# Scores of the two 16-wide attention layers: from 64x64 parts of the matmul array with four-head keys to 32x64 parts with two-head keys

## What is computed

```python
# layer 0
energy = jnp.einsum('bhqd,bhkd->bhqk', q, k)
att = jax.nn.softmax(energy, axis=-1) / D ** 0.5
out = jnp.einsum('bhqk,bhkd->bhqd', att, v)
# layer 3: the same with rotary q and k, and scores / sqrt(16)
```

## Time and profile before

| | us |
|---|---|
| runs | 2855.83, 2855.84, 2857.46 |
| median | 2855.84 |
| profiled execution, span from first to last instruction | 2859.8 |
| layer 0, tiles 5 to 28 (about) | 75 to 294 |
| layer 3, steady tiles | 2243 to 2468 |
| TensorE busy, whole span | 2583.2 (90%) |
| VectorE busy | 1614.8 (56%) |
| ScalarE busy | 1050.9 (37%) |
| GpSimd busy | 486.5 (17%) |
| mean granted TensorE clock | 0.962 of full |

### The profile page before, as it was taken

One profiled execution on the slowest core, in us unless ns is written; L12 is line 12 of the kernel. 1 busy time (PEld: TensorE's weight loads), 2 busy tenths in 40 slices (PEclk: granted clock), 3 DMA queues, 4 the chain that ended last, 5 costly groups with the idle time before them and its releaser, 6 DMA issues.

```text
span 2859.8 us, 60211 instructions
## 1 busy us (share of the span) xinstructions
PE 2583.2 (90%) x24161; PEld 1815.8 (63%) x24161; DVE 1614.8 (56%) x3691; ACT 1050.9 (37%) x2104; POOL 486.5 (17%) x407
## 2 busy tenths in 40 slices
PE   6888599999999946997999999997998888799999
PEld 5666366666666644665888888884444677556555
DVE  6999778787878773122455555443333677722221
ACT  4555365555555501211333333332121666411110
POOL 2223110101010103332111111110000656400000
PEclk9999899999999957998999999998998999999999
DMA  5000000000000032434100000000000233200000
GB/s 203 2 2 2 12 23 22 29 22 29 22 29 22 19 97 95 129 104 112 48 0 0 0 0 0 0 1 1 0 0 0 86 95 97 60 8 15 7 15 15
DMA packets 72121, 101.90 MB, mean 36 GB/s; under 512 B 10864, under 2 KB 50288, under 8 KB 71472
## 3 DMA queue, kind: packets, MB, share of 16 engines
q1 hardware_dynamic: 65840, 91.46, 10.0%
q0 software_dynamic: 6144, 8.56, 1.5%
HBM read 67.20 MB, written 32.80 MB: 35 GB/s over the span
## 4 chain that ended last, share of the span: by engine, by line
PE 79%; DVE 13%; issue 3%; ACT 2%; DMA 1%; POOL 1%; another core or an unknown queue 0%; SPq 0%; DVEq 0%; ACTq 0%
PE psW L320 16%; PE psW L313 8%; PE psS L1322 7%; PE psP L435 4%; PE psP L1288 4%; PE psP L428 4%; PE psP L1282 4%; PE psS L1316 4%; PE psO L1282 4%; PE psO L1288 4%; PE psS L379 3%; PE psO L412 3%; PE psO L344 2%; PE psW L528 2%; PE psP L395 2%
## 5 line engine op out<-in xcount | busy, mean ns | idle before, releaser
L320 PE MATMUL psW<-r,work 128*128 128x512 f32 x1024 | 481.6, 604 | 1.0 <-DVE work L755 1.0
L1218 POOL TENSOR_TENSOR work<-work 128x512 f32<-128x512 f32 x128 | 132.1, 1043 | 1141.8 <-DVE work L777 1141.7
L320 PEld LDWEIGHTS psW<-r,work 128*128 128x128 f32 x1024 | 180.6, 191 | 162.4 <-issue 156.8
L313 PE MATMUL psW<-work,r 128*128 128x128 f32 x2048 | 244.2, 278 | 1.0 <-DVE work L755 1.0
L313 PEld LDWEIGHTS psW<-work,r 128*128 128x128 f32 x2048 | 235.6, 193 | 3.5 <-DVE work L755 1.4
L766 DVE TENSOR_REDUCE work<-psS 128x8 f32<-128x512 f32 x256 | 175.4, 685 | 92.6 <-PE psS L558 55.8
L1322 PE MATMUL psS<-r,work 128*128 128x256 f32 x960 | 211.2, 381 | 5.3 <-DVE work L1385 5.3
L1322 PEld LDWEIGHTS psS<-r,work 128*128 128x128 f32 x960 | 181.2, 190 | 32.8 <-DVE work L1385 6.1
L768 DVE TENSOR_TENSOR work<-psS,work 128x512 f32<-128x512 f32 x256 | 176.9, 691 | 11.3
L1138 ACT ACTIVATE work<-work 128x512 f32<-128x512 f32 x128 | 80.1, 626 | 276.4 <-DVE work L768 276.4
L1196 POOL TENSOR_TENSOR work<-work,head_mask 128x1024 f32<-128x1024 f32 x64 | 121.2, 1894 | 207.0 <-ACT work L1074 204.5
(11 more groups left out here) (271 smaller groups left out, 4656.7 us busy)
## 6 DMA issues: line engine op xcount, KB each, us to landing
r<-in_l_fc SPq DMA_DIRECT2D x16, 1024.0 KB
rotated<-work SPq DMA_DIRECT2D x60, 256.0 KB
work<-mod_rows SPq DMA_DIRECT2D x64, 128.0 KB, 2.8
work<-rotated SPq DMA_DIRECT2D x30, 256.0 KB
r<-in_l_w SPq DMA_DIRECT2D x2, 3072.0 KB, 19.2
x<-in_x SPq DMA_DIRECT2D x8, 512.0 KB, 9.2
gather_table<-work SPq DMA_DIRECT2D x32, 128.0 KB, 1.8
moe_sum<-work SPq DMA_DIRECT2D x32, 128.0 KB, 1.7
```

Of the source, the lines that this page charges most:

```text
L313: ins = nc.tensor.matmul(ps[:, q * P:(q + 1) * P], w[:, k, lo + q * P:lo + (q + 1) * P], L.hT[:, k, :], start=(k == 0), stop=(k == KC - 1))
L320: ins = nc.tensor.matmul(ps[:, 0:width], L.hT[:, k, :], w[:, k, lo:lo + width], start=(k == 0), stop=(k == KC - 1))
L1218: nc.gpsimd.tensor_tensor(E, E, halves(L.rs)[i].unsqueeze(2).broadcast_to([P, 8, N]), ALU.mult).then_inc(L.s[f"prob{i}"].sem, 1)
```

## The change

The scores of layers 0 and 3 are computed on 32x64 parts of the array. One matmul now takes 32 partitions (two heads, "group" 0 to 3) and one sequence as weights and streams 128 columns: the 64 keys twice, each copy zeroed except for one of the two heads. That is 16 matmuls a tile where there were 8, each with half the rows and half the columns. The four groups write four banks: groups 0 and 1 the two banks of psP, groups 2 and 3 the two banks of psS, 256 columns in each. Since psP also receives the transposed probabilities, the scores of tile t now also wait for ptb of tile t-1.

`kbd` is halved (128x512), and so is its multiplication on GpSimd, which now takes its two 0/1 columns from `par`. VectorE has a softmax of its own for these layers: each of its four instructions takes the same 512 elements a partition as before, 256 from each of two banks (psP for the first half, psS for the second). The order of heads in E, and with it `narrow_pairs`, changes accordingly.

```diff
-                    self.kbd = [W.take(4, 4, N) for _ in range(2)]
+                    self.kbd = [W.take(4, 2, N) for _ in range(2)]
...
             for ch in range(KC):
-                for rh in range(2):
-                    for i in range(2):
-                        yield rh * 4 + ch * 2 + i, ch, rh * 2 + i
+                for group in range(4):
+                    yield group * 2 + ch, ch, group
...
                 after(pe, L.s["mask"], t + 1)
                 after(pe, L.s["sub1"], t)
+                after(pe, L.s["ptb"], t)
                 for ch in range(KC):
                     for b in range(2):
-                        for rh in range(2):
-                            rows, at = slice(64 * rh, 64 * rh + 64), rh * 512 + ch * 256
-                            bb = b ^ rh
-                            ins = nc.tensor.matmul(psS[64 * bb:64 * bb + 64, at:at + 256],
+                        for group in range(4):
+                            rows, bb = slice(32 * group, 32 * group + 32), b ^ (group % 2)
+                            ins = nc.tensor.matmul((psP, psS)[group // 2][64 * bb:64 * bb + 64, group % 2 * 512 + ch * 128:
+                                                                          group % 2 * 512 + ch * 128 + 128],
                                                    L.qk[t % 2][rows, ch, bb * N:(bb + 1) * N],
                                                    L.kbd[t % 2][rows, 2 * ch + bb, :, :], start=True, stop=True)
-                            if ch == KC - 1 and b == 1:
-                                ins.then_inc(L.s[f"s{rh}"].sem, 1)
+                            if ch == KC - 1 and b == 1 and group % 2:
+                                ins.then_inc(L.s[f"s{group // 2}"].sem, 1)
...
+        def dve_narrow_softmax(v, ch, L, t):
+
+            for i, ps in enumerate((psP, psS)):
+                ps = ps[:, :].rearrange("p (s a b) -> p s a b", s=2, b=N)[:, :, 0:4, :]
+                mx = halves(L.mx)[i].rearrange("p (s a) -> p s a", s=2)
+                after(v, L.s[f"s{i}"], t + 1)
+                ch.link(nc.vector.tensor_reduce(mx, ps, AX.X, ALU.max))
+                after(v, L.s["tb" if i else "ta"], t)
+                nc.vector.tensor_tensor(L.E[:, 8 * i:8 * i + 8, :].rearrange("p (s a) b -> p s a b", s=2), ps,
+                                        mx.unsqueeze(3).broadcast_to([P, 2, 4, N]), ALU.subtract
+                                        ).then_inc(L.s[f"sub{i}"].sem, 1)
...
-                nc.gpsimd.tensor_tensor(L.kbd[n % 2], k.unsqueeze(2).broadcast_to([P, 4, 4, N]),
-                                        head_mask[:, 8:12].unsqueeze(1).unsqueeze(3).broadcast_to([P, 4, 4, N]),
+                nc.gpsimd.tensor_tensor(L.kbd[n % 2], k.unsqueeze(2).broadcast_to([P, 4, 2, N]),
+                                        par.unsqueeze(1).unsqueeze(3).broadcast_to([P, 4, 2, N]),
                                         ALU.mult).then_inc(L.s["mask"].sem, 1)
```

More of the change, by code:

```diff
@@ L827, in dve_narrow @@
                 ch.reset()
-                dve_softmax(v, ch, L, t)
+                dve_narrow_softmax(v, ch, L, t)
                 if t > 1:
```

## The result

The changed kernel takes 2823.70 us (median of four runs, 2819.75 to 2826.11); the kernel before took 2856.65 us beside it (four runs, 2855.83 to 2859.12). The ratio is 0.988, with an interval of [0.9867, 0.9893]. Forecast were 2821 us, a range of 2797 to 2840, and 0.91 for faster. The profiled execution of the changed kernel took 2819.75 us, so it is the fastest of the four; its span is 2817.9.

What follows compares the result with a forecast made beforehand. VectorE, held by GpSimd's mask, bounds layer 0; TensorE's chain bounds layer 3. Savings of 20.4 + 2 + 12.6 = 35 us take the span from 2859.8 to 2824.8, median 4.0 lower: 2821 us, range 2797 to 2840.

Steps and rivals of the forecast that it cites:

- What bounds: Layer 0: VectorE, 96% busy, its normalisation held by GpSimd's mask, period 9.20 us; layer 3: TensorE's chain, 8.32 us.
- The mask: Layer 0: GpSimd's product falls to 1.04 us, VectorE's normalisation ends 0.85 us earlier in 24 tiles, 20.4 us.
- The ends of layer 0: The other eight tiles of layer 0: 0.4 us each for five, nothing for three; 2 us, bounds 0 and 5.
- The scores: Layer 3: eight parts at once cut the scores from 1.02 to 0.60 us; 0.42 in 30 tiles, 12.6 us.
- The sum: Whole kernel: 20.4 + 2 + 12.6 = 35 us saved, giving 2821 us, 1.2% less.
- Late next: Layer 3: whether VectorE becomes limiting; 0.85 of its 1.31 us wait before the softmax used up, 0.5 left.
- The edits at no cost: Wait for ptb, two-bank softmax halves, layer 3 mask, new narrow_pairs order: free, at worst 5 us over layer 0.
- A: Layer 3: only four parts work at once, so scores gain nothing; 22.4 us in all, 2833 us; chance 0.14.
- C: Layer 0 gains less: mask costs 1.28 us or two-bank softmax is slower; 24 to 29 us, 2829; chance 0.12.
- D: Scores slower: 32-row parts do not overlap, 3.7 us; layer 3 loses 80 us, layer 0 30; 2965; chance 0.05.
- E: Layer 0: the mask is not the cause of the 2.12 us normalisation; only 13 to 15 us remain, 2842; chance 0.03.
- B: Layer 0: normalisation escapes the mask after a 0.1 us shift, VectorE's loop 7.5 us; 56 us, 2800; chance 0.08.

Runs made afterwards that it cites:

- one column half: Changed kernel, but from tile 1 of each narrow layer all 16 score matmuls write the lower 64 partitions, four parts instead of eight; 2834.91 us, ratio 0.9920.
- half mask: Kernel before with its old scores, GpSimd masking only two of four head copies (512 elements) from tile 2 on; 2834.62 us, ratio 0.9926.
- the changed kernel again: Changed kernel unaltered, measured a second time beside the kernel before; 2819.25 us, ratio 0.9868.
- norm early: Layer 0's normalisation L743 moved ahead of the statistics, before the mask starts: on the changed kernel 2807.26 us, on the kernel before 2844.22 us.

## Why the prediction was right, point by point

**What bounds.** Both readings held. VectorE stays at 95% in layer 0, and TensorE's chain stays whole in layer 3. TensorE's loop in layer 0, put at 7.0 us, is the 7.08 to which tiles 25 to 28 fall once VectorE no longer binds. The two halves of the change, run alone, gave 20.9 us in layer 0 and 12.0 in layer 3 and add up to the whole; the prediction had costed them as two kernels in one, 22.4 and 12.6.

**The mask.** Taken was 1.04 us, from a product of as many elements with an operand that is constant inside; measured 1.040. The term 24 x 0.85 = 20.4 is 217.7 - 197.3 = 20.4 in the traces (tiles 5 to 28). The normalisation was expected at 1.27 and stands at 1.266 to 1.272 in 24 of 24.

**The ends of layer 0.** The estimate of 2 us was too low: the other seven intervals between scores went from 58.4 to 54.9, 3.5 us. It is the one term of the sum that was clearly mis-sized, within its bounds of 0 and 5.

**The scores.** Expected was 0.60 us for eight parts, 4 x 0.11 + 0.15; measured 0.62, and 1.03 for the same records on four parts, which is 8 x 0.11 + 0.15. The formula holds for both. The 0.15 for filling is a fit, though, and not every group has it: L583 sends its 32 records of 64 columns to four parts in 0.45 us, which is 8 x 0.056 with nothing added (its bursts of four start 0.056 us apart). It follows L578, whose parts have the same shape, while the scores follow a group on parts of another shape. That the filling belongs to the change of shape was not tried. The term of 12.6 us is 12.1 in the profile.

**The sum.** Forecast were 35 us, and the two layers gave 36.0. That is what can be held against the sum. That the median of 2823.70 also lies within 3 us of 2821 is partly luck: the same kernel gave 2819.25 later, and the stretch between the two layers, which the sum has at nothing, differs by several us from one execution to the next.

**Late next.** VectorE's reserve ahead of the softmax in layer 3 was put at 0.5; it is 0.56 and 1.05 in two tiles in a row. But the prediction let the rotated data arrive at a fixed time, and they don't: in some tiles the wait is zero and VectorE up to 0.7 us late. The period held even there, because the chain does not go through VectorE's softmax. So the conclusion was right, and this wait was not the measure of it.

**The edits at no cost.** The wait for ptb costs nothing: in the chain the scores follow L583 at once. The softmax over halves of two banks costs nothing: its maxima take 692 and 680 ns, its subtractions 691 and 691, where the means before were 685 and 691.

**The rivals.** *A* (four parts at once) has its price confirmed by the run with one column half: 15.7 us more than the change, of which 13.0 in layer 3. It did not happen. Neither did *C* and *D*. *E* (the mask is not the cause) fell with the half mask alone. *B* is the instructive one. I had priced it at 41 us in the 24 tiles of layer 0 if the normalisation slips out from under the mask, and had named a shift of a tenth of a microsecond as what would do it. The shift is right: a lead of 0.08 us is held, and one of 0.13 slips (the changed kernel again). The price is wrong. I had looked only at the instruction that was held, and not at what stands under the mask once it is gone. The changed kernel with the norm early is this rival's case: VectorE's loop is 7.93 us in tiles 5 to 24 and not 7.5, the 24 tiles take 187.1 us where they took 217.7, 30.6 less and not 41, and the time is 2807 and not 2800. The move alone gave 12.1 us where 24 x 0.86 would be 20.6. In the kernel before, with the longer mask, it gave 12.8 where 24 x 1.72 would be 41, since two steps on four columns were caught in its place. The lower edge of the range, taken from this rival, was thus some 7 us lower than it should have been.

**The rules weighed.** They are of the Trainium skill, page TensorE: Matmul & The Clock Gate. The section "Wait — 56ns, not 53.3ns?" gives some 25 ns from start to start of two matmuls, however small; here 32 records start within 0.43 us of each other, in bursts with 0.01 us between neighbours (the timeline of layer 0 above), and the link is 0.62 and not 0.95. The section "The mechanism" lets a weight load run under a matmul only of another row group; by it the move from eight parts to four, with the same four row groups, would have changed nothing, and it cost 0.41 us a tile. So for small matmuls that go to separate parts the rows decide against the floor as it stands there, and against my reading of the overlap rule as a limit on how many parts work at once; of matmuls on the whole array they say nothing. That the rows were followed is what made layer 3 come out.

## What to carry to other kernels

When an instruction takes five times what it takes elsewhere, line its end up with the ends on the other engines: 24 of 24 ends at the same distance to within a hundredth of a microsecond is as good as a semaphore in the program. Then shorten the one that holds, or put it where the held engine reads accumulators or computes statistics; moving the held instruction alone lets the next one be caught, and half (mask of 1.04 us) to three quarters (1.89 us) of the gain was lost so here. In this kernel small matmuls on parts of the array could be priced by records per part times the duration of one record, plus up to 0.2 us of filling, nearly whatever the order in the stream; and a faster stage is worth its gain only in the layer whose chain runs through it.

## What the runs showed of the hardware that I had not expected

- **Which instructions of VectorE wait for GpSimd.** Held until GpSimd's product ends, if they start 0.08 us ahead of it or under it: scalar, tensor-tensor and scalar-tensor-tensor operations on data in SBUF, however small (L743, L713 and L1691, L712). They end 0.15 us after it with 256 elements a partition and 0.02 us with four or eight. Not held, in the same places: the batch-norm statistics (0.41 to 0.43 us in every position), sums over data in SBUF (L1690, 0.69 us), and the instructions that read an accumulator (maximum, subtraction, reciprocal, residual addition), which take as long under a GpSimd product as without one. I have not tried why the two kinds differ.
- **The hold goes both ways.** A normalisation that starts 0.13 or 0.22 us ahead of the mask takes its 0.41 us, and the mask takes 0.14 or 0.05 us more than usual; with a lead of 0.08 us it is the normalisation that is held.
- **Eight parts of the array at once.** 32 records of 128 columns, float32, pass in 0.62 us, and in 1.03 on four parts; neighbours in a burst start 0.01 us apart.
- **Order in the stream.** Four records of one part in a row, eight times over, cost 0.06 us against an order that changes part after every two.
- **A short dip of the clock that cost nothing.** With the old mask and the new scores the granted clock fell for some 3 us in five tiles of layer 0 (means of 0.56 to 0.70 of full over the 3 us), and once in the kernel before (0.66 from 122 to 125 us). The long tile was made good by a short one: 10.52, 7.65 and 9.21 us are 27.4 together, where three regular tiles of 9.19 are 27.6. What sets off the dip was not tried.
